# First projection of the queries and keys: by row tile instead of by block, with the query masks on three engines

## What is computed

```python
xn = _layernorm(x, axis=-1)
x = x + attn(xn, Wq, Wk, Wv, Wo, g) + ffn(xn, W1, b1, W2, b2)
# attn: 16 heads, q and k of 16 features, v of 64
#   A = tril(taylor_exp(q) . taylor_exp(k)), y = A @ v
#   y = y * rsqrt(mean(y*y)) * g, out = y @ Wo.T
#   taylor_exp(x) = [1, x/2, outer(x, x)/(4*sqrt(2))]
# ffn: gelu(xn @ ternary(W1).T + b1) @ ternary(W2).T + b2
```

## Time and profile before

| what | value |
|---|---|
| median of 3 executions | 760.08 us (760.06 to 760.13) |
| the profiled execution | 760.95 us |
| its span, slowest core (5) | 759.2 us |
| spans of the 8 cores | 753.8 to 759.2 us |
| TensorE busy on core 5 | 691.8 us, 91% |

### The profile page before, as it was taken

One profiled execution on the slowest core, in us unless ns is written; L12 is line 12 of the kernel. 1 busy time (PEld: TensorE's weight loads), 2 busy tenths in 40 slices (PEclk: granted clock), 3 DMA queues, 4 the chain that ended last, 5 costly groups with the idle time before them and its releaser, 6 DMA issues.

```text
span 759.2 us, 11498 instructions; the slowest of 8 cores (753.8 to 759.2 us)
## 1 busy us (share of the span) xinstructions
PE 691.8 (91%) x4050; PEld 335.8 (44%) x4050; DVE 417.8 (55%) x623; ACT 243.4 (32%) x322; POOL 99.1 (13%) x131
## 2 busy tenths in 40 slices
PE   2777888877789888999999999999999999999998
PEld 1344544544445444444444444444444444444443
DVE  6667564678577566276556435351554554401653
ACT  3456666657557443222333333333100000000000
POOL 3112222224122211000000001010010000000000
PEclk9999999999999999999999999999999999999999
DMA  7974464766848624659786614533353676200883
GB/s 155 204 161 103 87 122 92 171 146 194 216 143 261 201 69 128 171 198 303 216 281 175 213 56 131 200 114 110 111 200 133 206 223 195 98 1 20 244 232 115
DMA packets 65415, 121.49 MB, mean 160 GB/s; under 512 B 22096, under 2 KB 28112, under 8 KB 65360
## 3 DMA queue, kind: packets, MB, share of 16 engines
q1 hardware_dynamic: 46752, 64.46, 28.0%
q0 software_dynamic: 18608, 56.30, 27.2%
HBM read 103.30 MB, written 16.78 MB: 158 GB/s over the span
## 4 chain that ended last, share of the span: by engine, by line
PE 81%; ACT 6%; DMA 5%; issue 4%; DVE 2%; POOL 2%; SPq 0%; ACTq 0%; DVEq 0%; POOLq 0%
PE pST L1199 8%; PE pY L1221 7%; PE pSS L1199 7%; PE pST L1221 7%; PE pW L1199 7%; PE pW L1221 7%; PE pSS L1221 7%; PE pY L1199 7%; PE pSS L977 4%; PE pW L1134 4%; PE pW L977 4%; PE pSS L1134 3%; ACT Am L922 3%; DMA xr<-x 2%; PE pSS L966 2%
## 5 line engine op out<-in xcount | busy, mean ns | idle before, releaser
L1221 PE MATMUL pY<-w2t,hT 128*128 128x512 bf16 x256 | 66.0, 379 | 0.1
L1221 PE MATMUL pST<-w2t,hT 128*128 128x512 bf16 x256 | 66.0, 379 | 0.0
L1221 PE MATMUL pSS<-w2t,hT 128*128 128x512 bf16 x256 | 66.0, 379 | 0.0
L1221 PE MATMUL pW<-w2t,hT 128*128 128x512 bf16 x256 | 66.0, 379 | 0.0
L524 POOL TENSOR_SCALAR_AFFINE_SELECT Am<-Am 128x1024 bf16<-128x1024 bf16 x32 | 35.3, 1104 | 208.4 <-ACT Am L922 208.4
L1199 PE MATMUL pST<-xnT,w1t 128*128 128x512 bf16 x272 | 61.5, 379 | 0.0
L1199 PE MATMUL pSS<-xnT,w1t 128*128 128x512 bf16 x256 | 57.9, 379 | 0.4 <-DVE consts L705 0.4
L1199 PE MATMUL pW<-xnT,w1t 128*128 128x512 bf16 x256 | 57.9, 379 | 0.0
L1199 PE MATMUL pY<-xnT,w1t 128*128 128x512 bf16 x240 | 54.2, 379 | 0.0
L719 DVE TENSOR_SCALAR w1t<-stg,consts 128x2048 bf16<-128x2048 f32 (+1 forms) x18 | 21.0, 1165 | 54.1 <-PE pY L1199 53.9
L517 POOL DMA_DIRECT2D stg<-w1r x32 | 25.1, 784 | 163.3 <-DVE w1t L722 147.5
(11 more groups left out here) (185 smaller groups left out, 1043.0 us busy)
## 6 DMA issues: line engine op xcount, KB each, us to landing
stg<-w1r POOLq DMA_DIRECT2D x32, 1024.0 KB, 7.5
stg<-w2r SPq DMA_DIRECT2D x16, 1024.0 KB, 9.0
stg<-w2r POOLq DMA_DIRECT2D x16, 1024.0 KB, 7.1
xr<-x SPq DMA_DIRECT2D x16, 512.0 KB, 5.2
res_scr<-rst SPq DMA_DIRECT2D x16, 512.0 KB, 3.2
res<-res_scr SPq DMA_DIRECT2D x32, 256.0 KB, 3.6
xs<-x SPq DMA_DIRECT2D x32, 256.0 KB, 3.9
out<-osb SPq DMA_DIRECT2D x32, 256.0 KB, 2.5
```

What stands on the lines that cost most here:

```text
L1221: return e.matmul(out_bank(n), hT[:, j, 128 * t:128 * t + 128], w2t[8 * dh + j // 4][:, j % 4, :], start=(j == 0), stop=(j == NJ - 1))
```

## The change

1. Weights: GpSimd asks for `wqk` behind tile 0 of x and for `wv` behind tile 1.
2. VectorE: `ln_b(0)` stands ahead of `ln_a(1)`, and `ln_b(1)` ahead of `ln_a(2)`.
3. TensorE: block 0 is projected tile by tile. `first(t)` takes one turned tile and makes 16 matmuls of 128 columns, 8 for the queries and 8 for the keys; these stand between the turns. Queries and keys lie in the two banks of one pair (`pW`); the turns use `pST` and `pY` in alternation, so turns 2 and 3 wait for tiles 0 and 1 to be copied out.
4. VectorE empties the queries and masks heads 0 to 3; ScalarE empties the keys and masks heads 4 and 5; GpSimd masks heads 6 and 7. `scores(0)` waits for all three.
5. The small query squares of block 0 move to the end of step 0. Their reader, `y_before(1)`, waits for them. The table of units has one unit less in front, so in step 0 the pairs of banks are exchanged.

```diff
-EMPTIED_BY = {"q": "D", "k": "D", ...
+EMPTIED_BY = {"q": "D", "k": "A", ...
-            return (None, None, ("qk", 1), ("qg", 1))[ph]
+            return (("qg", 0), None, ("qk", 1), ("qg", 1))[ph]
-    order = [("q", 0), ("k", 0), ("qg", 0)]
+    order = [("q", 0), ("k", 0)]
+PAIR_NO[UID[("q", 0)]] = PAIR_NO[UID[("k", 0)]] = PAIR_NO[UID[("s", 0)]]
+M_DVE, M_ACT = 4, 6
-    TURN = (pW, pSS, pST, pY)
+    TURN = (pST, pY, pST, pY)
...
-        for t in range(3):
-            dX.wait_done(e, t)
+        dX.wait_done(e, 0)
         e.dma_start(out=wqk[:, 0, :, :], in_=wqk_d[0]).then_inc(dQK[0], 16)
-        dX.wait_done(e, 3)
+        dX.wait_done(e, 1)
         for n in range(2):
             e.dma_start(out=wv[:, 0, 4 * n:4 * n + 4, :],
...
+        q_ready(e, 0)
+        for h in range(M_ACT, 8):
+            e.tensor_scalar(qblk[:, 0, h, :], qkT[:, 0, 0, :], hmask[:, h:h + 1], None,
+                            ALU.mult).then_inc(gQM, 1)
...
         ln_a(0)
+        ln_b(0)
         ln_a(1)
-        ln_b(0)
+        ln_b(1)
         ln_a(2)
-        ln_b(1)
         ln_a(3)
...
-        empty_first("q", 0)
+        unit_filled(e, ("q", 0))
+        e.tensor_copy(qkT[:, 0, 0, :], bank(("q", 0))).then_inc(dW, 1)
         q_ready(e, 0)
-        for h in range(8):
+        for h in range(M_DVE):
...
-        empty_first("k", 1)
...
+        unit_filled(e, ("k", 0))
+        e.copy(qkT[:, 0, 1, :], bank(("k", 0), 1)).then_inc(aW, 1)
+        q_ready(e, 0)
+        for h in range(M_DVE, M_ACT):
+            e.activation(qblk[:, 0, h, :], qkT[:, 0, 0, :], AF.Copy,
+                         scale=hmask[:, h:h + 1]).then_inc(aQM, 1)
         e.wait_ge(sMS, 3)
-        empty_side(("qg", 0))
...
+        def first(t):
+            turned(e, t)
+            for half, kind in enumerate("qk"):
+                dst = bank((kind, 0), half)[:, 128 * t:128 * t + 128]
+                for kd in range(KD):
+                    mm = e.matmul(dst, wqk[:, 0, kd, 128 * half:128 * half + 128],
+                                  xnT[:, t, kd, :], start=(kd == 0),
+                                  stop=(kd == KD - 1))
+                if t == T_PE - 1:
+                    mm.then_inc(pWU, 1)
...
-                    e.wait_ge(dQM, 8)
+                    e.wait_ge(dQM, M_DVE)
+                    e.wait_ge(aQM, M_ACT - M_DVE)
+                    e.wait_ge(gQM, 8 - M_ACT)
...
         for t in range(T_PE):
+            if t >= 2:
+                turned(e, t - 2)
             turn(TURN[t][:], t).then_inc(pT, 1)
-        first("q", 0)
-        first("k", 128)
-        side(("qg", 0))
+            if t == 1:
+                e.wait_ge(dQK[0], 16)
+            if t >= 1:
+                first(t - 1)
+        first(T_PE - 1)
```

More of the change, by code:

```diff
@@ L27 @@
 SBUF_BASE = 16512
-EMPTIED_BY = {"q": "D", "k": "D", "qk": "D", "qg": "A", "qv": "A", "s": "A",
+EMPTIED_BY = {"q": "D", "k": "A", "qk": "D", "qg": "A", "qv": "A", "s": "A",
               "vk": "A", "v": "A", "kx": "A", "q2": "A", "vv": "A", "v1": "A", "t": "A",
@@ L319, in build_program @@
     sA1 = S("sA1"); sA1D = S("sA1D"); sA2 = S("sA2"); aG = S("aG")
-    dQM = S("dQM"); dW = S("dW"); dKF = S("dKF"); dRD = S("dRD"); dRC = S("dRC")
+    dQM = S("dQM"); aQM = S("aQM"); gQM = S("gQM"); dW = S("dW"); dKF = S("dKF"); dRD = S("dRD"); dRC = S("dRC")
     dNM = S("dNM"); dS1 = S("dS1"); sTR = S("sTR"); sTH = S("sTH"); sTC = S("sTC")
@@ L633, in vec_stream @@
         assert su[0] == N_SETUP
-        def empty_first(kind, half):
-            unit_filled(e, (kind, 0))
-            e.tensor_copy(qkT[:, 0, half, :], bank((kind, 0))).then_inc(dW, 1)
         def empty_qk(B):
```

## The result

The changed kernel takes 763.76 us in the median of 13 executions (761.63 us the quickest), the kernel before beside it 760.13 us. The ratio is 1.0056, with a 95% interval from 1.0036 to 1.0076: slower by 0.56%, some 4.2 us. The forecast was no change at 759.8 us, with a range up to 762.2 us; both were wrong. One execution of each kernel, 848 and 872 us long, ran with disturbed cores and counts in no comparison.

The account below looks back on a forecast made before the run. TensorE was busy for 91% of slowest core 5's span. A start gain of 1.4 us less 1.1 us for the squares gave 0.3 us earlier: 760.65 us profiled, 759.8 us median, range 757.2 to 762.2 us.

Parts of the forecast that it names:

- The weights: Start-up: `wqk` asked for at 8.15 us, landing 7.2 us later at 15.3 us, 2.6 us earlier; bounds 15.3 to 16.5 us.
- TensorE's order: Block 0's projections and turns: 80 matmuls of 128 columns from 15.3 us, ending at 22.3 us; bounds 21.6 and 23.7 us.
- From the last projection to the scores: Queries' copy and masks ahead of the first scores: 2.8 us, bounds 2.4 and 3.5 us; scores at 25.3 us, 1.9 us earlier.
- The clock behind the gap: First values, behind TensorE's idle time: a possible fall to 1.2 GHz costs 1.7 us; start gain taken as 1.4 us.
- The squares: Small query squares on ScalarE, between `ysq` and step 1's `Am`: cost 1.1 us, bounds 1.0 to 1.2 us.
- VectorE's order and the bank exchange: Start-up normalisation reordered, priced at nothing; in step 1 the exchange moves `scores(1)` by 0.9 us, hidden beneath the squares.
- a shift of the start passes nearly whole: From step 0 to the kernel's end: a start-up shift should reach the end nearly whole, since the feed-forward stages run densely.
- the slower one: Rival at the first two values: the clock falls in the gap with nothing gained before; 1.4 us slower, chance 0.22.
- Six masks in turn: Rival at the masks: VectorE's and GpSimd's six run in turn, 2.2 us instead of 1.5 us; 760.5 us, chance 0.1.
- The weights are not earlier: Rival at the start: `wqk` and x share engines, landing at 17 us or later; 1.7 us lost, 761.5 us, chance 0.05.
- The rival of the late stall: Rival at a late weight load and the output projection: the slowest core loses its bad stall; 757.5 us, chance 0.2.

Follow-up runs that it names:

- no_pool: The changed kernel with heads 0 to 5 masked by VectorE, 6 and 7 by ScalarE, none by GpSimd; ratio 1.001 to the kernel before.
- mid_np: The changed kernel with heads 0 to 5 masked by VectorE, 6 and 7 by ScalarE, and the squares directly behind the first `Am`; ratio 0.9994 to before.
- b_sq: The kernel before with only the small query squares moved to the end of step 0; ratio 1.0053 to the kernel before.
- b_w: The kernel before with only the earlier requests for `wqk` and `wv` and VectorE's new order; ratio 1.0017 to the kernel before.
- tile_only: The changed kernel with all eight masks on VectorE and the small query squares back ahead of the first scores; ratio 0.9994 to the kernel before.

## Why the prediction was wrong

By its own steps:

- **The weights.** The request came at 8.1 us as said. The landing was priced at 7.2 us; the first projection started at 16.47 us on core 5. SP's request for tile 4 of x, which waits for `wqk`, stood at 16.75 us on average over the cores before (14.96 to 19.04 us) and stands at 16.13 us now (14.62 to 18.36 us). The mean over the cores went from a request at 10.36 us to one at 8.08 us, so 2.3 us of earlier request brought 0.6 us. From request to landing it was 6.4 us on average before and 8.1 us now. One core's duration was taken for all, and it was taken to stay as it was; why it grew, no run shows.
- **TensorE's order.** The last projection was to end between 21.6 and 23.7 us, with 22.3 us in the sum. On core 5 it ended at 24.05 us, outside these bounds; the first one had started 1.2 us later than the 15.3 us of the sum. The keys' projection before ended at 25.9 us, so 1.8 us were gained where 3.6 us were counted on. And the queries, which the masks need, are not ready earlier at all: VectorE's copy of them gained 0.13 us on average of the eight cores.
- **From the last projection to the scores.** This step failed in its price, and most of the loss follows from it: 2.8 us, bounds 2.4 and 3.5 us, measured 4.07 us on every core. The scores start at 28.12 us on core 5, where the sum had 25.3 us; 1.75 us of the difference are the later end of the projections, 1.1 us this gap. GpSimd's mask was taken at 0.55 us, at the rate of its triangle, and its upper bound at the whole triangle's 1.09 us; it costs 1.56 us. VectorE's masks at 0.48 us instead of 0.27 us did not matter, and ScalarE's 1.33 us for two was near the 1.2 us taken.
- **The clock behind the gap.** The mechanism was right, the size was not: taken as half a fall, it came on all 8 cores, behind 4.07 us of idle time. With 2.6 us of it, it came on 3 (no_pool) or 6 (mid_np). The values' stretch grew by 1.67 us on average, the 1.7 us that rows 8 and 9 gave.
- **The squares.** 1.1 us was taken for the wait; 1.24 us is what step 2 shows in the changed kernel, and by the mean core they cost 1.4 to 2.0 us. The sum had missed that this wait, too, brings the clock down (3 cores here, 7 in b_sq).
- **VectorE's order and the bank exchange** cost nothing that shows in the changed kernel, where turn 3 stands behind the wait for `wqk`. In b_w, where the turns do not wait for the weights, the new order makes tile 3 0.3 us later, so it is not free by itself.

Added up over the eight cores: copy -0.13, wait +0.46, values' stretch +1.67, step 2 +1.24, together 3.24 us; the cores reach the up projection 3.4 us later (302.46 against 299.08 us), and the spans are 3.1 to 3.8 us longer. Against the forecast, the scores are the largest miss: 1.9 us earlier in the sum, 0.3 us later as measured. For this pair the loss is whole at 42 us and passes to the end. It is no rule: tile_only starts the values of step 2 1.5 us later than before and reaches the up projection 0.3 us earlier. So the prediction's premise that a shift of the start passes nearly whole is shown for this change only, and the shares of the loss above are those of one execution.

Among the rivals, the slower one named the right mechanism and place. Its price of a fall, 1.7 us, was right. Its total of 1.4 us was too low because it still counted on a start 1.4 us earlier; it had a chance of 0.22. "Six masks in turn" was wrong: GpSimd is nearly as slow without VectorE's masks, and the two engines' masks overlap. "The weights are not earlier" was half right: 0.6 us earlier on average, and landed only beyond 18 us on core 1. The rival of the late stall is not shown: the slowest core is some 3 us above the mean core before and after. Its counterargument, that the stall comes each time since three executions agreed within 0.07 us, rested on luck: twelve executions of the kernel before spread from 759.05 to 761.40 us.

## What to carry to other kernels

Price an operation on GpSimd from a row of the same operation; one of another kind was off by a factor of three here. Work that is free stays free only where its engine waits: before moving it, look at what its engine does at the new place, and whether TensorE waits there. And when TensorE is to wait in a chain that is not dense, count the clock's fall as part of the price: here it came on 0 to 7 of 8 cores with waits of some 2 us, and on 8 of 8 with 4 us. But expect less than its full price back from filling the gap.

## What the runs showed of the hardware

- `tensor_scalar` with a column as the factor, 128x512 bf16: 1.56 us on GpSimd without VectorE's masks, 1.64 us on average beside them; 0.27 us on VectorE, 0.48 us on average beside GpSimd's; some 0.65 us on ScalarE as a scaled copy (six in 3.78 us). GpSimd cuts a triangle of twice the size in 1.09 us.
- The clock fell with an idle stretch of 4.07 us ahead of the scores on 8 of 8 cores, of 2.6 us on 3 of 8 in one kernel and on 6 of 8 in another (mid_np), and of 0.5 us on none. A single short matmul at the start of the wait did not keep it up (tile_only, 2.24 us behind it, 7 of 8), while cores 1, 2 and 7 of the kernel before had 2.0 us idle and no fall. So the length of the last idle stretch alone does not decide it.
- Idle matmuls held the clock up (no early falls in three kernels), yet the gain in the mean core was 0.1 to 0.8 us, each good to about 0.3 us, where the stretch behind them had won 0.6 to 1.9 us.
